# Retention by token tile: decay in the rotary tables, the state summed in PSUM, first network weights loaded during it

## The chip, the core and the metric

The program runs on one core of one Trainium2 chip. The core has five engines that run their own instruction queues and meet only at semaphores: TensorE (PE in the profile; PEld is its loading of stationary operands), VectorE (DVE), ScalarE (ACT), GpSimd (POOL) and SyncE (SP), which here only issues transfers (DMAs). The metric is the device time of one execution in microseconds (us).

## What is computed

`x` is 4 x 512 x 128 float32 (4 batches, 512 tokens, 128 columns). Three parts follow one another: a retention layer with four heads, a local-attention network of six layers, and a second layer (attention and a mixture of experts). The first part is what is rewritten:

```python
xn = layernorm(x)
s, g = retention(xn), silu(network(xn))                 # then x + s * g goes into the second layer
# retention(x), for x = xn:
normed = (x - mu) * rsqrt(var + EPS) * ln_w + ln_b
q, k, v, g = normed @ Wq, normed @ Wk, normed @ Wv, normed @ Wg
q, k = rope(q) * dk ** -0.5, rope(k)                    # dk = 32
def step(S, inp):                                       # per head, over chunks of tokens
    attn = (q @ k.T) * Dmask                            # Dmask = gamma ** (i - j), 0 for j > i
    o = attn @ v + (q * cross) @ S                      # cross = gamma ** (i + 1)
    S = S * gC + (k * kdec).T @ v                       # gC, kdec: powers of gamma
o = o * rsqrt(mean(o ** 2) + EPS) * g_norm_w * silu(g)  # per head
out = x + o @ Wo
```

So there are two norms in a row. The once normed x, transposed, is `state` in the kernel: the retention's product is added to it, and the network starts from it.

## The kernel before, in words

The program is three blocks, one after the other, and every engine meets the others at a barrier between them: `build_retention` (lines 802 to 1206), `build_network` (from 51) and `build_second_layer`.

In the retention, tokens lie 128 to a tile: four tiles (t) of 128 tokens, each for all four batches at once. First come the two norms over all 16 token tiles in two halves (lines 1131 to 1145 on VectorE, 1056 to 1064 on ScalarE), with TensorE transposing x, the once normed x and the twice normed x (954). Then a hardware loop runs over the four tiles; the first three turns are the loop, the last stands behind it. In one turn `project` (982) makes q and k, the gate and v; `rotate` (1163 to 1169) turns q and k and multiplies q by the decay; GpSimd multiplies k by its decay (940) and the gate by the norm weights (944); TensorE transposes q, k and decayed q (990 to 998), makes scores (1012), the state's increment (1003), the product with the state (1021) and the product with v (1027). VectorE applies the decayed mask (1175), blocks out the state's increment (1181) and adds it to the decayed state (1188). ScalarE squares the output (1093), VectorE sums (1185), ScalarE makes the inverse root by Ln and Exp (1095, 1097), VectorE multiplies twice (1190, 1194), TensorE transposes (1036) and multiplies by Wo (1040), VectorE adds `state` (1200). The eight banks of PSUM are four fixed pairs (pa to pd), each reused several times in a turn, so that a step waits until the pair is read out.

In the network's block, SyncE issues the tables and the first layer's weights as its first instructions (220 to 232), GpSimd makes the scaled rotary tables from them (287), VectorE sets constants (666 to 676), and TensorE waits for those constants and for the weights before its first product (384). VectorE's first rotation (716) waits for GpSimd's tables. Each engine's order is written out by hand, stage by stage.

Of the kernel before, what the change touches and what calls it, by code (L numbers as in the profile page):

```python
# [59 lines left out]
def build_network(nc, w_qkv, w_o, w_1, w_2, cols, qk_scale, rotary, win_mask, state):  # L60
# [3 lines left out]
    with ctx:  # L64
# [13 lines left out]
        mask_f = sb("mask_f", [P, 2, 2 * WIN])  # L78
        rot_base = sb("rot_base", [P, 4, TILES, DH])
        rot = sb("rot", [P, 2, 4, TILES, DH])  # L80
        qks = sb("qks", [P, DEPTH * 4, DH])
        wqkv = sb("wqkv", [P, 3 * INNER])
        wo = sb("wo", [P, PAIRS, P])
        w1 = sb("w1", [P, 2 * FF])
        w2 = sb("w2", [P, 3, P])
        col = sb("col", [P, 9])
# [35 lines left out]
        s_const = sig("s_const")  # L122
        s_wq, s_wk, s_wv = sig("s_wq"), sig("s_wk"), sig("s_wv")
        s_qks, s_wo, s_wffn = sig("s_qks"), sig("s_wo"), sig("s_wffn")
        v_moved = [sig(f"v_moved{t}") for t in range(TILES)]
        moves_of = [16 * (16 - 2 * (t == TILES - 1)) for t in range(TILES)]
        c_ident, c_dve, rot_ready = sig("c_ident"), sig("c_dve"), sig("rot_ready")
# [88 lines left out]
        with nc.Block() as block:  # L216

            @block.sync
            def _(sp):
                sp.dma_start(mask_f[:, :, :], win_mask).then_inc(s_const, 16)  # L220
                sp.dma_start(rot_base[:, :, :, :], rotary).then_inc(s_const, 16)

                def load_qkv(l, k, signal):
                    sp.dma_start(half(wqkv, k), w_qkv[l, :, INNER * k:INNER * (k + 1)]).then_inc(signal, 16)

                def load_out(l):
                    sp.dma_start(wo[:, :, :], w_o[l, :, :].rearrange("p (c n) -> p c n", n=P)).then_inc(s_wo, 16)

                def load_ffn(l):
                    sp.dma_start(w1[:, :], w_1[l, :, :]).then_inc(s_wffn, 16)  # L230
                    sp.dma_start(w2[:, :, :], w_2[l, :, :].rearrange("p (c n) -> p c n", n=P)).then_inc(s_wffn, 16)
                    sp.dma_start(col[:, :], cols[l, :, :]).then_inc(s_wffn, 16)

                load_qkv(0, 0, s_wq)
                load_qkv(0, 1, s_wk)
                load_qkv(0, 2, s_wv)
                sp.dma_start(qks[:, :, :].rearrange("p k d -> p (k d)"), qk_scale.to_broadcast([P, DEPTH * 4 * DH])).then_inc(s_qks, 16)
                load_out(0)
                load_ffn(0)

                for g in range(TILE_COUNT):
# [3 lines left out]
                    if last_of_layer:  # L245

                        sp.wait_ge(k_full, 2 * (g + 1))
                        load_qkv(l + 1, 1, s_wk)
                        sp.wait_ge(q_full, 2 * (g + 1))
                        load_qkv(l + 1, 0, s_wq)  # L250
                        sp.wait_ge(v_full, 2 * (g + 1))
                        load_qkv(l + 1, 2, s_wv)
# [13 lines left out]
                    if l > 0 and b == 0 and t == TILES - 1:  # L266

                        sp.wait_ge(wo_full, 2 * r)
                        load_out(l)
                    if l > 0 and b == 1 and t == 2:  # L270

                        sp.wait_ge(x_ffn, 2 * (r - 1))
                        load_ffn(l)

            @block.gpsimd
            def _(pool):
# [4 lines left out]
                pool.wait_ge(s_const, 32)  # L281
                pool.wait_ge(s_qks, 16)

                def tables(l):

                    for k in range(4):
                        ins = nc.gpsimd.tensor_tensor(rot[:, l % 2, k, :, :], rot_base[:, k, :, :],  # L287
                                                      qks[:, 4 * l + k:4 * l + k + 1, :].to_broadcast([P, TILES, DH]), ALU.mult)
                    ins.then_inc(rot_ready, 1)

# [37 lines left out]
                tables(0)  # L328
                for g in range(TILE_COUNT + 2):
# [14 lines left out]
                    if g % (B * TILES) == 2 and l + 1 < DEPTH:  # L344

                        tables(l + 1)
# [455 lines left out]
def build_retention(nc, state, x0T, sT, x, w_ret, w_ro, ret_cols, g_norm, ret_rot, ret_decay, ret_diag, ret_block):  # L802

# [3 lines left out]
    with ctx:  # L807
# [3 lines left out]
        def sig(name, per=1, start=0):  # L811
            return Signal(ctx, nc, name, per, start)


        pa = ctx.enter_context(nc.psum_tensor("pa", [P, 2, 512], F32))
        pb = ctx.enter_context(nc.psum_tensor("pb", [P, 2, 512], F32))
        pc = ctx.enter_context(nc.psum_tensor("pc", [P, 2, 512], F32))
        pd = ctx.enter_context(nc.psum_tensor("pd", [P, 2, 512], F32))

        ident = sb("r_ident", [P, P])  # L820
        eps_col = sb("r_eps_col", [P, 1])
        primer = sb("r_primer", [P, 2])
# [3 lines left out]
        gnw = sb("gnw", [P, 2 * P])  # L826
        rrot = sb("rrot", [P, 2, TILES, RK])
        rdec = sb("rdec", [P, 2, P])
        rdiag = sb("rdiag", [P, RH, P])
        rblock = sb("rblock", [P, 2 * P])  # L830

        xtok = sb("r_xtok", [P, BT, P])
        xc = sb("r_xc", [P, BT, P])
        sqs = sb("r_sqs", [P, BT, P])
        xn = sb("r_xn", [P, BT, P])
        nr = sb("r_nr", [P, BT, P])
        msum = sb("r_msum", [P, BT])
        mean = sb("r_mean", [P, BT])
        vsum = sb("r_vsum", [P, BT])
        var = sb("r_var", [P, BT])  # L840
        lnv = sb("r_lnv", [P, BT])
        rstd = sb("r_rstd", [P, BT])
        nrT = sb("nrT", [P, B, T])

        nrc = sb("nrc", [P, B, P])
        rt1 = sb("rt1", [P, B, 2 * P])
        rt2 = sb("rt2", [P, B, 2 * P])
        rqk = sb("rqk", [P, B, 2 * P])
        qcr = sb("qcr", [P, B, P])
        kst = sb("kst", [P, B, P])  # L850
        vsb = sb("vsb", [P, B, 2 * P])
        sg = sb("sg", [P, B, 2 * P])
        sgn = sb("sgn", [P, B, 2 * P])
        rT = sb("rT", [P, 3, B, P])
        at = sb("at", [P, RH, B, P])
        st = sb("st", [P, B, 2 * P])
        stn = sb("stn", [P, B, 2 * P])
        osq = sb("osq", [P, B, 2 * P])
        oss = sb("oss", [P, B * RH])
        oln = sb("oln", [P, B * RH])  # L860
        orst = sb("orst", [P, B * RH])
        o1 = sb("o1", [P, B, 2 * P])
        o2 = sb("o2", [P, B, 2 * P])
        orT = sb("orT", [P, 2, B, P])

        loads = [(wr[:, :], w_ret), (wro[:, :, :], w_ro), (rcol[:, :], ret_cols), (rrot[:, :, :, :], ret_rot),
                 (rdec[:, :, :], ret_decay), (rdiag[:, :, :], ret_diag), (rblock[:, :], ret_block)]
        all_loads = 16 * (len(loads) + 1)
        c_loads = sig("r_loads")
        r_ident = sig("r_identity")  # L870
        c_set = sig("r_set")
        x_in = [sig("r_x_in_0"), sig("r_x_in_1")]

        steps = sig("r_steps")
        centred = sig("r_centred", 2)
        squared = sig("r_squared", 2)
        stats = sig("r_stats", 2)
        ln_there = sig("r_ln_there", 2)
        rstd_there = sig("r_rstd_there", 2)
# [38 lines left out]
        with nc.Block() as block:  # L918
# [32 lines left out]
            def _(pe):  # L951
# [33 lines left out]
                def retain(t, more):  # L985
# [45 lines left out]
                    if more:  # L1031
                        project(t + 1)
# [1061 lines left out]
```

## Time and profile before

| | us |
|---|---|
| median of 3 runs (1910.48 to 1913.82) | 1913.39 |
| the profiled execution | 1910.66 |
| its span, first to last instruction | 1908.8 |
| PE busy / DVE / ACT / POOL | 1773.3 / 1479.6 / 1179.6 / 1199.0 |

The span is what the trace covers; 1.86 us of the profiled execution's time lie outside it. Busy shares are means over three stages of unlike kind: the retention ends at 133.94 us, the network's steady run lasts until about 1700 us, and the second layer fills the rest. In rows of the timeline, the two first numbers are the start and the duration in us, `xN` counts records, and the bracket gives the idle time before and what ended it. One matrix product in float32 leaves two records in the trace.

### The profile page before, as it was taken

What the parts mean: (1) busy time and instruction counts of PE and PEld (TensorE: products, weight loads), DVE (VectorE), ACT (ScalarE), POOL (GpSimd) and SP (SyncE); (2) the same over time, 40 slices, a digit from 0 to 9 for tenths busy, and PEclk for the clock granted to TensorE, in tenths of its full rate; (3) what the DMA queues carried; (4) which work ended last, traced back from release to release, by engine and by line L of the source; (5) the groups of instructions that cost most, each with busy time, mean ns of one, the idle gap of its engine ahead of it and who ended that gap; (6) DMA issues with size and microseconds to landing.
All of it is one profiled execution on the core that took longest, in us unless ns stands there. A gap on an engine that the chain in (4) does not pass through costs nothing. (4 is left out here: it accounts for less than half of the span.)

```text
span 1908.8 us, 70807 instructions
## 1 busy us (share of the span) xinstructions
PE 1773.3 (93%) x30380; PEld 1139.9 (60%) x30380; DVE 1479.6 (78%) x1676; ACT 1179.6 (62%) x2045; POOL 1199.0 (63%) x1291
## 2 busy tenths in 40 slices
PE   5867899999999999999999999999999999998689
PEld 4743566656665665665566566666656656665356
DVE  6547787887888878788887888888788887876276
ACT  4324666676667657667665766766676666665374
POOL 0108867777776777677677767777776776773000
PEclk9979999999999999999999999999999999999799
DMA  1013322332322322222323223223223222221022
GB/s 50 0 61 91 74 58 66 75 89 67 79 68 58 98 69 73 65 69 66 93 70 77 67 56 103 67 71 78 69 56 91 68 73 72 69 65 27 30 46 67
DMA packets 87379, 128.45 MB, mean 67 GB/s; under 512 B 26616, under 2 KB 32640, under 8 KB 87072
## 3 DMA queue, kind: packets, MB, share of 16 engines
q1 hardware_dynamic: 87072, 123.97, 25.8%
q8 instruction: 240, 3.93, 0.9%
q14 instruction: 67, 0.55, 0.1%
HBM read 25.24 MB, written 1.11 MB: 14 GB/s over the span
## 5 line engine op out<-in xcount | busy, mean ns | idle before, releaser
L317 POOL TENSOR_TENSOR qkn<-t 128x1024 f32<-128x1024 f32 x192 | 453.8, 2364 | 313.1 <-DVE t L720 312.5
L308 POOL TENSOR_TENSOR qkn<-qkn,rn 128x512 f32<-128x512 f32 x384 | 398.2, 1068 | 14.7 <-POOL rn L302 1.3
L444 PEld LDWEIGHTS sc_ps<-prT,v_win 64*64 64x64 f32 x12288 | 198.2, 135 | 147.8 <-issue 146.9
L584 ACT ACTIVATE sq<-qk_ps 128x1024 f32<-128x1024 f32 x192 | 196.0, 1021 | 100.4 <-PE qk_ps L384 98.6
L399 PE MATMUL ring<-ident,qkn 128*128 128x128 f32 x1536 | 242.2, 280 | 10.9 <-POOL qkn L308 10.0
L399 PEld LDWEIGHTS ring<-ident,qkn 128*128 128x128 f32 x1536 | 176.7, 141 | 124.2 <-issue 76.0
L325 POOL TENSOR_TENSOR pn<-pexp,rden 128x512 f32<-128x512 f32 x192 | 196.5, 1045 | 74.2 <-DVE rden L704 74.2
L716 DVE TENSOR_TENSOR t<-qk_ps,rot 128x1024 f32<-128x1024 f32 x192 | 229.4, 1195 | 16.9 <-POOL rot L287 8.6
L577 ACT COPY prT<-ring 128x512 f32<-128x512 f32 x192 | 111.2, 579 | 200.4 <-PE ring L428 199.9
L720 DVE TENSOR_TENSOR t<-qk_ps,rot 128x1024 f32<-128x1024 f32 x192 | 232.9, 1213 | 0.0
L730 DVE TENSOR_REDUCE sums<-sq 128x16 f32<-128x1024 f32 x192 | 232.2, 1209 | 0.0
L444 PE MATMUL sc_ps<-prT,v_win 64*64 64x32 f32 x12288 | 219.2, 221 | 4.1 <-DVE pr L692 3.4
L414 PEld LDWEIGHTS sc_ps<-kT,qT 64*32 64x32 f32 x12288 | 138.1, 105 | 107.5 <-issue 73.6
L374 PE MATMUL qk_ps<-wqkv,state 128*128 128x512 f32 x384 | 197.2, 596 | 0.0
L391 PE MATMUL ring<-wqkv,state 128*128 128x512 f32 x384 | 196.3, 593 | 0.0
L414 PE MATMUL sc_ps<-kT,qT 64*32 64x64 f32 x12288 | 170.3, 224 | 23.7 <-ACT oT L549 12.8
L384 PE MATMUL qk_ps<-wqkv,state 128*128 128x512 f32 x384 | 182.6, 598 | 10.3 <-DMA wqkv<-in_w_qkv 8.5
L683 DVE TENSOR_TENSOR sc_ps<-sc_ps,mask_f 128x1024 f32<-128x1024 f32 x96 | 118.3, 1233 | 86.2 <-PE sc_ps L414 85.4
L459 PE MATMUL ring<-oT,wo 128*128 128x256 f32 x768 | 174.7, 381 | 0.0
L549 ACT COPY oT<-sc_ps 128x512 f32<-128x512 f32 x192 | 112.9, 589 | 70.9 <-PE sc_ps L444 70.9
L459 PEld LDWEIGHTS ring<-oT,wo 128*128 128x128 f32 x768 | 143.0, 191 | 17.7
L738 DVE TENSOR_TENSOR xa<-ring,state 64x256 f32<-64x256 f32 x96 | 40.6, 423 | 136.3 <-PE ring L459 134.9
(223 smaller groups left out, 2808.8 us busy)
## 6 DMA issues: line engine op xcount, KB each, us to landing
v_win<-v_tok SPq DMA_DIRECT2D x1488, 64.0 KB
wqkv<-in_w_qkv SPq DMA_DIRECT2D x18, 512.0 KB, 3.6
spread<-gate_rows SPq DMA_DIRECT2D x32, 128.0 KB, 3.8
wo<-in_w_o SPq DMA_DIRECT2D x6, 512.0 KB, 3.8
w<-in_w SPq DMA_DIRECT2D x6, 341.0 KB, 3.3
w<-in_w SPq DMA_DIRECT2D x6, 192.0 KB, 2.9
r_xtok<-in_x SPq DMA_DIRECT2D x4, 256.0 KB, 3.7
out_x<-xo SPq DMA_DIRECT2D x4, 256.0 KB, 2.2
```

What stands on the lines that cost most here:

```text
L308: nc.gpsimd.tensor_tensor(by_head(quarter(qkn, f)), by_head(quarter(qkn, f)), rn[:, 8 * f:8 * (f + 1)].unsqueeze(2).to_broadcast([P, 8, DH ...
L317: nc.gpsimd.tensor_tensor(half(qkn, k), half(t1, k), half(t2, k), ALU.add).then_inc((q_added, k_added)[k], 1)
L325: nc.gpsimd.tensor_tensor(by_head(quarter(pn, f)), by_head(quarter(pe_, f)), rden[:, 8 * f:8 * (f + 1)].unsqueeze(2).to_broadcast([P, 8, D ...
L374: nc.tensor.matmul(qk_ps[:, f, :], tile_of(g), quarter(wqkv, f), start=True, stop=True).then_inc(q_full, 1)
L391: nc.tensor.matmul(ring_bank("v", g, f), tile_of(g), quarter(wqkv, 4 + f), start=True, stop=True).then_inc(v_full, 1)
L399: ins = nc.tensor.transpose(to[:, n * P:(n + 1) * P], qkn[:, c * P:(c + 1) * P], ident[:, :])
L414: ins = nc.tensor.matmul(sc_ps[WIN * q:WIN * (q + 1), par, 64 * pair:64 * (pair + 1)], qT[64 * par:64 * (par + 1), pair, WIN * q:WIN * (q ...
L444: ins = nc.tensor.matmul(sc_ps[64 * par:64 * (par + 1), part, P * pair + WIN * q:P * pair + WIN * (q + 1)], v_win[64 * part:64 * (part + 1 ...
L459: ins = nc.tensor.matmul(to[:, 0:2 * P], wo[:, c, :], oT[:, c, 2 * P * f:2 * P * (f + 1)], start=(c == 0), stop=(c == PAIRS - 1))
L716: nc.vector.tensor_tensor(by_head(half(t1, k)), by_head(of), rot[:, l % 2, 2 * k, s:s + 1, :].to_broadcast([P, HEADS, DH]), ALU.mult).then ...
L720: nc.vector.tensor_tensor(half(t2, k).rearrange("p (h s d) -> p h s d", s=2, d=DH // 2), swapped, rot[:, l % 2, 2 * k + 1, s:s + 1, :].to_ ...
L730: nc.vector.tensor_reduce(sums[:, HEADS * k:HEADS * (k + 1)], by_head(half(sq, k)), AX.X, ALU.add).then_inc(sums_ready, 1)
```

## The change

The diff changes the first block and moves the first loads of the second. In words:

- The decay powers go into the rotary tables: q's table holds `gamma ** (n - 255.5) * dk ** -0.5`, k's holds the inverse power, for n over all 512 tokens. A plain causal mask replaces the decayed one, and the state needs no decay: its increments are summed in two PSUM banks (`held`) over the tiles, and VectorE only blocks them out into SBUF before each product.
- The norms are made per tile, and the second norm's variance is worked out from the first (`second_variance`). The weights `g_norm_w` are multiplied into Wo once (`scale_weights`). The decay of q and k and the gate's weighting on GpSimd are gone. The sum of the two rotated terms is on VectorE, as before.
- The loop is gone: 36 uses of two pairs of PSUM banks are listed in one order (`fills`), and each engine's queue is written out over all four tiles.
- ScalarE sets the table for Ln and Exp once, at the start; the loads behind it are put in by the build. Line 1091, which set it again in every tile, is gone.
- SyncE issues the network's tables and first weights in the retention's block, and GpSimd makes the first rotary tables there.
- In the second layer two waits (`gated`, `a_max`) become the helper `then`, which waits in the same place on another semaphore.

```diff
+class NetworkWeights:
+    def load_tables(self, sp):
+        sp.dma_start(self.mask_f[:, :, :], self.win_mask).then_inc(self.s_const, 16)
+        sp.dma_start(self.rot_base[:, :, :, :], self.rotary).then_inc(self.s_const, 16)
+        sp.dma_start(self.qks[:, :, :].rearrange("p k d -> p (k d)"), self.qk_scale.to_broadcast([P, DEPTH * 4 * DH])).then_inc(self.s_qks, 16)
...
 def build_retention
+                load_x(0)
+                load_x(1)
+                for to, of in first_loads:
+                    sp.dma_start(to, of).then_inc(c_first.sem, 16)
+                load_x(2)
+                load_x(3)
+                for to, of in later_loads:
+                    sp.dma_start(to, of).then_inc(c_later.sem, 16)
+                weights.load_tables(sp)
+                for k in range(3):
+                    weights.load_qkv(sp, 0, k)
+                weights.load_out(sp, 0)
+                weights.load_ffn(sp, 0)
...
+                def update(t):
...
+                    for b in range(B):
+                        ins = nc.tensor.matmul(held[:, b // 2, 256 * (b % 2):256 * (b % 2 + 1)], rqk[:, t % 2, b, P:2 * P], vsb[:, t % 2, b, :],
+                                               start=(t == 0 and b % 2 == 0), stop=(b % 2 == 1), skip_group_check=True)
...
+                def second_deviation(t):
+                    act.wait_ge(v2_there.sem, t + 1)
+                    nc.scalar.activation(ln2[:, t, :], v2[:, t, :], ACT.Ln, bias=rcol[:, 2:3]).then_inc(logs.sem, 1)
+                    log_taken()
+                    nc.scalar.activation(rstd2[:, t, :], ln2[:, t, :], ACT.Exp, scale=-0.5).then_inc(rstd2_there.sem, 1)
...
+                def inverse_norms(t):
+                    act.wait_ge(r_ms.sem, t + 1)
+                    nc.scalar.activation(oln[:, t % 2, :], oss[:, t % 2, :], ACT.Ln, bias=rcol[:, 2:3], scale=1.0 / RV).then_inc(logs.sem, 1)
+                    log_taken()
+                    if t >= 2:
+                        act.wait_ge(r_o.sem, t - 1)
+                    nc.scalar.activation(orst[:, t % 2, :], oln[:, t % 2, :], ACT.Exp, scale=-0.5).then_inc(r_orst.sem, 1)
...
+                def rotate(t, k):
...
+                    if k == 0:
...
+                        nc.vector.tensor_tensor(rt1[:, :, :], of, table, ALU.mult)
+                    else:
+                        for s in range(2):
+                            ins = nc.vector.tensor_tensor(heads(rt2[:, :, :])[:, :, :, s, :], heads(of)[:, :, :, 1 - s, :], heads(table)[:, :, :, s, :], ALU.mult)
+                        ins.then_inc(r_terms.sem, 1)
+                def add_terms(t):
...
+                    nc.vector.tensor_tensor(rqk[:, t % 2, :, :], rt1[:, :, :], rt2[:, :, :], ALU.add).then_inc(r_rot.sem, 1)
+                def masked(t, k):
...
+                                            rmask[:, :].unsqueeze(1).to_broadcast([P, 2 * B, P]), ALU.mult).then_inc(r_at.sem, 1)
...
 def build_network
-                load_qkv(0, 0, s_wq)
-                load_qkv(0, 1, s_wk)
-                load_qkv(0, 2, s_wv)
-                load_out(0)
-                load_ffn(0)
...
-                tables(0)
```

Three places in the engines' queues show what moves. The first is TensorE's queue in the retention. Before, this is one turn of the loop from the scores on (`at` is the masked scores, `st` the state, `nrc` the normed input, `o` the gated output):

```order
L1012 MATMUL pa<-rT 128x128 x8
L1012 MATMUL pc<-rT 128x128 x8
L1016 REGISTER_ALU
L1003 MATMUL pb<-vsb,kst 128x256 x2
L1021 MATMUL pd<-st,rT 128x256 x4
L1027 MATMUL pd<-vsb,at 128x64 x8
L982 MATMUL pa<-wr,nrc 128x256 x4
L982 MATMUL pc<-wr,nrc 128x256 x4
L982 MATMUL pb<-wr,nrc 128x256 x4
L1036 MATMUL pd<-r_ident,o 128x128 x8
L1040 MATMUL pd<-orT,wro 128x512 x2
```

Now, in the middle of the same engine's queue (`rqk` is rotated q and k, `r_held` the summed state, `nr` and `xn` the twice and once normed x):

```order
L1036 MATMUL r_out_ps<-vsb,at 128x64 x16
L989 MATMUL r_ring<-r_ident,rqk 128x128 x8
L966 MATMUL r_ring<-r_ident,r_nr 128x128 x4
L972 MATMUL r_ring<-r_ident,r_xn 128x128 x4
L1013 MATMUL r_held<-vsb,rqk 128x256 x4
L981 MATMUL r_ring<-wr,nrc 128x256 x12
L1024 MATMUL r_out_ps<-st,rT 128x256 x4
L966 MATMUL r_ring<-r_ident,r_nr 128x128 x4
L981 MATMUL r_ring<-wr,nrc 128x256 x4
```

Before, only the next tile's projection stands between a tile's output and its transposes; now work of three tiles stands there, and a tile's last steps come a tile or more later.

The second is ScalarE's queue at the retention's end. Before, from the last tile's transposed scores' operands to the barrier:

```order
L1090 COPY rT<-pd 128x512 x2
L1090 COPY rT<-pb 128x512
L1091 ACT_TABLE_LOAD
L1093 ACTIVATE osq<-pd 128x1024
L1095 ACTIVATE oln<-oss,r_eps_col 128x16
L1097 ACTIVATE orst<-oln 128x16
L1102 COPY orT<-pd 128x512 x2
L918 UNCONDITIONAL_BRANCH
```

Now, the same stretch (`oln` is the logarithm of the summed squares `oss`, `orst` the inverse root):

```order
L1188 ACT_TABLE_LOAD
L1188 ACTIVATE oln<-oss,rcol 128x16
L1192 ACT_TABLE_LOAD
L1192 ACTIVATE orst<-oln 128x16
L1184 ACTIVATE osq<-r_out_ps 128x1024
L1198 COPY orT<-r_ring 128x1024
L1188 ACT_TABLE_LOAD
L1188 ACTIVATE oln<-oss,rcol 128x16
L1192 ACT_TABLE_LOAD
L1192 ACTIVATE orst<-oln 128x16
L1198 COPY orT<-r_ring 128x1024 x2
L900 UNCONDITIONAL_BRANCH
```

Where one load stood ahead of both functions, one now stands ahead of each; over the retention ScalarE has eleven loads and had nine.

The third is SyncE's queue around the barrier (the branches) between retention and network. Before:

```order
L925 DMA rblock<-in_ret_block 128x256
L926 DMA gnw<-in_g_norm 128x256
L918 UNCONDITIONAL_BRANCH
L218 UNCONDITIONAL_BRANCH
L220 DMA mask_f<-in_win_mask 128x128
L221 DMA rot_base<-in_rotary 128x1024
L224 DMA wqkv<-in_w_qkv 128x1024 x3
L237 DMA qks<-in_qk_scale 128x1536
L227 DMA wo<-in_w_o 128x1024
```

Now:

```order
L914 DMA wro<-in_w_ro 128x256
L914 DMA gnw<-in_g_norm 128x2
L86 DMA mask_f<-in_win_mask 128x128
L87 DMA rot_base<-in_rotary 128x1024
L88 DMA qks<-in_qk_scale 128x1536
L91 DMA wqkv<-in_w_qkv 128x1024 x3
L94 DMA wo<-in_w_o 128x1024
L900 UNCONDITIONAL_BRANCH
L258 UNCONDITIONAL_BRANCH
L281 DMA v_win<-v_tok 32x512
```

All of the network's first loads now stand ahead of the barrier, behind the retention's own loads.

## Rows read from the trace of the kernel before

**Rows 1.** The page: the span, first to last instruction.

```profile
span 1908.8 us, 70807 instructions
```

**Rows 2.** Stretches A:B: length, busy us (records) per engine, PEclk, DMA share, GB/s.

```profile
51.00:74.00 23.00, 19.79 (x131) 16.46 (x130) 14.19 (x14) 8.79 (x12) 4.09 (x2) 1.00 0.00 0
...
120.20:134.00 13.80, 5.75 (x12) 2.73 (x12) 6.15 (x6) 2.68 (x5) 0.00 (x0) 0.62 0.00 0
134.00:147.20 13.20, 6.17 (x11) 2.83 (x12) 1.23 (x8) 2.88 (x4) 3.27 (x6) 0.62 0.81 305
147.20:1700.00 1552.80, 1500.72 (x28084) 947.48 (x28083) 1276.65 (x1359) 1016.13 (x1776) 1145.91 (x1235) 1.00 0.29 72
```

**Rows 3.** Timeline of one tile, 51 to 74 us: start, duration, engine, line, operation.

```profile
51.18 1.02 ACT L1093 ACTIVATE osq<-pd 128x1024 f32<-128x1024 f32 x1 [7.99 <-PE pd L1027]
52.24 1.22 DVE L1185 TENSOR_REDUCE oss<-osq 128x16 f32<-128x1024 f32 x1 [4.53 <-ACT osq L1093]
53.49 0.31 ACT L1095 ACTIVATE oln<-oss,r_eps_col 128x16 f32<-128x16 f32 x1 [1.29 <-DVE oss L1185]
54.06 1.28 ACT L1083 ACT_TABLE_LOAD   x1
55.36 1.02 ACT L1083 ACTIVATE sg<-pc 128x1024 f32<-128x1024 f32 x1
...
57.10 0.86 PEld L1036 LDWEIGHTS pd<-r_ident,o 128*128 128x128 f32 x8 [1.12 <-DVE o L1194]
...
58.92 1.98 PE L1040 MATMUL pd<-orT,wro 128*128 128x512 f32 x4 [0.73 <-ACT orT L1102]
...
61.21 1.40 DVE L1200 TENSOR_TENSOR sT<-pd,state 64x512 f32 x2
...
64.99 1.37 PE L1012 MATMUL pa<-rT 32*128 32x128 f32 x13
...
67.74 1.13 PE L1003 MATMUL pb<-vsb,kst 128*128 128x256 f32 x4
...
68.71 1.89 PE L1021 MATMUL pd<-st,rT 128*128 128x256 f32 x8
...
70.43 3.68 PE L1027 MATMUL pd<-vsb,at 128*128 128x64 f32 x32
73.95 1.95 PE L982 MATMUL pa<-wr,nrc 128*128 128x256 f32 x8
```

**Rows 4.** Timeline of the start, 0 to 36 us.

```profile
4.51 1.22 DVE L1136 TENSOR_REDUCE r_msum<-r_xtok 128x8 f32<-128x1024 f32 x1 [2.36 <-DMA r_xtok<-in_x]
...
12.40 0.17 DVE L1142 TENSOR_SCALAR r_var<-r_vsum 128x8 f32<-128x8 f32 x1
...
16.84 1.92 PE L954 MATMUL pd<-r_ident,r_xn 128*128 128x128 f32 x8
...
24.40 2.35 ACT L1072 COPY state<-pc 64x512 f32<-64x512 f32 x4
...
32.05 3.35 PE L982 MATMUL pa<-wr,nrc 128*128 128x256 f32 x8 [3.53 <-DVE nrc L1152]
```

**Rows 5.** Transfers of the first 12 us: count, KB each, median us from issue to landing.

```profile
wr<-in_w_ret SPq DMA_DIRECT2D x1, 384.0 KB, 4.9
```

**Rows 6.** Timeline of the retention's end and the network's start, 132 to 148 us.

```profile
132.53 1.41 DVE L1200 TENSOR_TENSOR sT<-pd,state 64x512 f32<-64x512 f32 x2 [6.51 <-PE pd L1040]
...
138.34 0.23 DVE L676 TENSOR_SCALAR centre_w<-ident 128x128 f32<-128x128 f32 x1 [2.77 <-DMA rot_base<-in_rotary]
...
141.03 3.47 PE L384 MATMUL qk_ps<-wqkv,state 128*128 128x512 f32 x4 [8.53 <-DMA wqkv<-in_w_qkv]
...
144.34 2.77 POOL L287 TENSOR_TENSOR rot<-rot_base,qks 128x256 f32<-128x256 f32 x4 [9.46 <-DMA qks<-in_qk_scale]
...
147.21 1.22 DVE L716 TENSOR_TENSOR t<-qk_ps,rot 128x1024 f32<-128x1024 f32 x1 [8.64 <-POOL rot L287]
```

**Rows 7.** A stretch at the retention's end, columns as in rows 2.

```profile
123.60:134.00 10.40, 5.75 (x12) 2.73 (x12) 3.76 (x5) 1.17 (x2) 0.00 (x0) 0.50 0.00 0
```

More of the change, by code:

```diff
@@ L63, in build_network @@
+def build_network(nc, weights, state):
     ctx = ExitStack()
@@ L344, in _ @@
                     if g % (B * TILES) == 2 and l + 1 < DEPTH:
-                        tables(l + 1)
+                        weights.scale_rotary(nc, l + 1)
             @block.tensor
@@ L851, in build_retention @@
[L851 to L863, printed above, removed]
@@ new lines, in turn_qk, with scores @@
+                def turn_qk(t):
+                    pe.wait_ge(r_rot.sem, t + 1)
+                    free("turn", t)
+                    for k in range(2):
+                        for b in range(B):
+                            ins = nc.tensor.transpose(banks_of("turn", t)[:, k, P * b:P * (b + 1)], rqk[:, t % 2, b, P * k:P * (k + 1)], ident[:, :])
+                    ins.then_inc(r_turned.sem, 1)
+                def scores(t, k):
+                    if k == 0:
+                        pe.wait_ge(r_T.sem, t + 1)
+                    what = ("low", "high")[k]
+                    free(what, t)
+                    for h in (2 * k, 2 * k + 1):
@@ L1065, in _ @@
-                for n, banks in ((1, (pc, pd)), (2, (pa, pb))):
-                    for half in range(2):
-                        act.wait_ge(turned.sem, turned.at(n, half + 1))
-                        for b in range(2 * half, 2 * half + 2):
-                            if n == 1:
-                                for late, rows in enumerate(HALVES):
-                                    first = b * SHIFTED + late
-                                    ins = nc.scalar.copy(state[rows, first:first + T], banks[half][rows, b % 2, :])
-                            else:
-                                ins = nc.scalar.copy(nrT[:, b, :], banks[half][:, b % 2, :])
-                        ins.then_inc(copied.sem, 1)
@@ new lines, in copy_state @@
+                def copy_state(t):
+                    act.wait_ge(s_turned.sem, t + 1)
+                    if t == 0:
+                        act.wait_ge(c_set.sem, B)
+                    for late, rows in enumerate(HALVES):
+                        ins = nc.scalar.copy(state[rows, :].rearrange("p (b n) -> p b n", b=B)[:, :, P * t + late:P * (t + 1) + late],
+                                             banks_of("ln", t)[rows, 1, :].rearrange("p (b n) -> p b n", b=B))
+                    ins.then_inc(s_copied.sem, 1)
```

812 lines of the change are left out of this document (487 added, 325 removed).

## The prediction

> **What bounds the kernel now.** I read the page first [rows 1], then the busy time by stage, since shares over the whole span mix three stages. In the network's steady stretch TensorE is busy 1500.72 of 1552.80 us [rows 2]: nothing there is touched, and a network that starts earlier ends earlier by the same time. The retention is another case. It ends at 132.53 + 1.41 = 133.94 us [rows 6], and one of its tiles takes 23.00 us, of which TensorE is busy 19.79, VectorE 14.19 and ScalarE 8.79 [rows 2]. The timeline of that tile shows why TensorE isn't full: squares (51.18), sum (52.24), Ln (53.49), two products on VectorE, transposes (57.10), Wo (58.92), the sum with `state` (61.21) run one behind the other on four engines, each engine waiting for the last [rows 3]. Behind the last tile stand 13.80 us with TensorE busy for 5.75 [rows 2]. Ahead of the first tile stand 32.05 us of norms. Then the network waits for its own loads: its first product is at 141.03, behind 8.53 us of idleness that ended with the transfer of `wqkv`, its first rotation at 147.21, behind GpSimd's tables, which waited for `qks` [rows 6].
>
> **The change part by part: the retention.** Every tile's work now lies beside that of two others, so I take the durations of the old rows and lay them out in the new queues, each instruction behind its engine's last one and behind what it waits for, with 0.05 us for a signal between engines. TensorE's prices at the pace of the tile in rows 3, from start to start: a group of four 128x256 products (a projection, the state's increment, the product with the state) 70.43 - 68.71 = 1.72; the 16 score products 67.74 - 64.99 = 2.75; the 16 products with v 73.95 - 70.43 = 3.52; eight transposes 0.86; the two products with Wo 1.72 (four records at 0.43, the 1.98 less the tail of the last). VectorE: 1.22 per 1024 columns, 0.70 per 512 (two in 1.40), 0.17 for a small one [rows 3, 4]. ScalarE: 1.02 per 1024, 0.59 per 512 (four in 2.35), a table load 1.28, Ln 0.31 [rows 3, 4].
>
> First, up to the first dense stretch of TensorE. Tile 0 of x is there at about 4.4 (4.51 before, for two transfers [rows 4]). Mean, centring and square to 7.0; VectorE centres tile 1 meanwhile, then variance, root, second variance and second root to 10.1; VectorE is then busy with tile 2, and the twice normed tile stands at 11.9. Transposes and copy to 13.9, and q and k by 17.9, at the low pace (below). Rotation with its sum, and tile 1's norm among it, to 22.4; transposes of q and k wait for a copy of `state` on ScalarE until 25.1, and tile 0's v starts at 26.5, when tile 1's q and k are read out of the bank that it wants. Tables and weights of the retention do not hold this up: the last that tile 0 needs is issued as the sixth transfer, at about 3.3, and with the 4.9 us of `wr` [rows 5] lands by about 8.2, near the first Ln.
>
> Second, the dense stretch, from tile 0's v to tile 3's product with v. The queue holds ten projections (17.2), eight half-tiles of scores (11.0), four products with v (14.1), three increments and three products with the state (10.3), three transposes of q and k (2.6), tiles 2 and 3 normed (1.7), one transposed output (0.9) and one Wo (1.7): 59.5. Waits that the other engines cause in it: 0.3 + 0.4 + 0.2 + 0.5 + 0.2, together 1.5. VectorE has about 16 us of work per tile and ScalarE 13 with its loads, where TensorE has 18.7, so neither is late for long. End: 26.5 + 59.5 + 1.5 = 87.5.
>
> Third, the tail. ScalarE squares the last tile to 89.2, copies tile 1's output to 90.2, loads a table to 91.5, Ln, loads another, Exp to 93.3, copies tile 2's output to 94.4. Wo of tile 2 and transposes of tile 3 to 97.2, copy to 98.3, Wo to 100.3, two sums to 101.8. The tail, 14.3 us, is as long as before: the two loads that stand in it take what the overlap gives. So the retention ends at 101.8 instead of 133.94: 32.1 us off.
>
> **Clock.** At the start, eight transposes took 1.92 at 16.84 and a projection 3.35 at 32.05 [rows 4], against 0.86 and 1.72 in the tile [rows 3]: that is 1.2 GHz against 2.4. Behind the last tile, after TensorE had waited since 120.2, the granted clock was 0.50, the lower level [rows 7]. I take the low level for all of TensorE's work until 17 us, when the first projection is through. If the low pace lasted until 30 us, the same layout ends at 107.0; with the high one from the start, at 99.2. The Trainium skill, page "TensorE: Matmul & The Clock Gate", Part 4 "PE-mode transpose", says that transposes don't count as busy time for that clock. The trace agrees as far as it goes: transposes that followed others without a gap still ran at the low pace [rows 4]. By that rule the many transposes in the new start would keep the low pace longer, which is the 107.0; it is rival B.
>
> **ScalarE's loads.** The change has two more loads, but what counts is where they stand: one between Ln and Exp, in the chain. The load took 1.28 and the next operation began 0.02 behind its end [rows 3]. With no cost for loads the layout ends at 99.5, with twice the row, as if the engine had to empty first, at 110.6. The page "ScalarE: Activation LUTs" of the Trainium skill, section "What ACT_TABLE_LOAD costs", gives a load of about 1.28 us and as much again for draining, about 2.66 together. I go by the row; the page's price is rival C.
>
> **The network's start.** What remains ahead of the first product is VectorE's constants. They were done at 138.34 - 2.77 = 135.57 (the idle time before `centre_w` [rows 6]), 1.63 behind the retention's end; with `centre_w` (0.23) and a signal TensorE starts 1.91 behind it instead of 7.09. Four records at the low pace take 3.47 as before [rows 6], and the squares 1.02, so the first rotation comes 6.5 behind the end instead of 147.21 - 133.94 = 13.3: 6.8 off. At the high pace it would be 8.5. I take the low pace, since TensorE has waited 3 us by then, in a thin tail. GpSimd's 2.77 us of tables lie in the retention, where GpSimd has only four other operations. Transfers: 3.9 MB queue behind the retention's own and stand in nobody's way, since the retention's own are issued first; its last table tile is wanted at 24 us. Bounds: 0 (they land too late) to 8.5.
>
> **Second layer.** The two waits keep their places and what they wait for: 0. Beside the network nothing else changes: its queues are those of before, with other line numbers.
>
> **Sum.** 32.1 + 6.8 = 38.9 off. Against the profiled execution's own time (the span of 1908.8 [rows 1] and 1.86 outside it, 1910.66) that is 1871.8; that execution lies 2.7 below the median of the runs, from which the sum gives 1874.5. I say 1873.
>
> **Rivals.**
> A, the layout holds, with a microsecond or three more or less in the waits between engines: 1870 to 1877. Chance 0.70.
> B, TensorE stays at the low level until the dense stretch at 30 us: 5.2 later, 1878. For it: its work comes in short pieces in the first 25 us, much of it transposes. Against: a projection of 3.4 us and transposes stand together at 12 to 17 us. 0.10.
> C, each table load costs twice its row: 8.8 later, 1882. Against it stands the row. 0.04.
> D, the change doesn't do what it says at the barrier: the network's first rotation still comes 13 us behind the retention, because something else than loads is late there. 6.8 later, 1880. For it: two waits, TensorE's for `wqkv` and GpSimd's for `qks`, ended at different times, so a third may lie under them. Against: constants are all that is left in the queues. 0.06.
> E, the high level from the start and at the network's start: 2.6 and 1.7 earlier, 1869. 0.06.
> F, slower than before: TensorE holds the low level through the retention, as its work now waits in small pieces on other engines. Then TensorE's queue alone sets the time and the retention ends at 168.3, 66.5 later: 1939. It decides once the low pace lasts until about 100 us, where the layout ends at 140.4, the 133.94 plus what the network's start gives back. Against it: the old tile, with TensorE busy for 19.79 of 23.00, kept a granted clock of 1.00 [rows 2], and the new stretch is denser. 0.04.
>
> **How the numbers follow.** 1873 is A's. The range 1863 to 1888 takes in B to E, and room for signals that cost 0.1 us rather than 0.05 (2 us later) or waits with several signals. A difference under 0.2% (3.8 us) can't be told from none here. All but F are far below 1909.6: faster 0.95, no change 0.01, slower 0.04.
>
> **What would show it.** Right: the last sum into `sT` ends at 100 to 104 us; from 26 to 87 TensorE has no gap over 1 us; the four tiles' products with v end near 35, 59, 70 and 88 us; Ln and Exp of a tile with 1.28 between them; the first rotation 6 to 7 us behind the retention's end with no wait on a transfer. Wrong: granted clock at 0.50 past 30 us, gaps over 1 us in the dense stretch that end with VectorE or ScalarE, or a network whose steady stretch is not 1553 us long.

## The result, and the profile after

The changed kernel takes 1883.59 us (median of four runs, 1881.55 to 1887.45) against 1912.72 of the kernel before (four runs): ratio 0.9852, 95% interval 0.9837 to 0.9867. That is 29.1 us off, where the forecast had 38.9 by its sum and 1873 as its number. The profiled run is the longest of the four, 1887.45.

The page of the changed kernel, the row that answers to [rows 1]:

```profile
span 1885.3 us, 70702 instructions
```

The end of the retention and the network's start, changed kernel (start us, us, engine, line, operation), answering to [rows 6]:

```profile
102.52 1.28 ACT L1188 ACT_TABLE_LOAD   x1
103.81 0.31 ACT L1188 ACTIVATE oln<-oss,rcol 128x16 f32<-128x16 f32 x1
104.14 1.28 ACT L1192 ACT_TABLE_LOAD   x1
...
112.65 1.41 DVE L1355 TENSOR_TENSOR sT<-r_ring,state 64x512 f32<-64x512 f32 x2 [2.55 <-PE r_ring L1054]
...
116.07 3.14 PE L392 MATMUL qk_ps<-wqkv,state 128*128 128x512 f32 x4 [3.46 <-DVE centre_w L684]
...
120.47 1.23 DVE L724 TENSOR_TENSOR t<-qk_ps,rot 128x1024 f32<-128x1024 f32 x1 [4.49 <-ACT sq L592]
```

The last sum into `sT` ends at 112.65 + 1.41 = 114.06, against 133.94 before and 101.8 forecast. The network's first product now waits for VectorE's `centre_w` and for no transfer, and its first rotation comes 120.47 - 114.06 = 6.41 behind the retention's end, where it was 13.27. So the network starts its rotations 147.21 - 120.47 = 26.7 us earlier. From there to the last masked score of the network (1726.92 here, 1750.73 before) the two profiles need 1606.45 and 1603.52, and from that score to the end of the span 158.4 and 158.1: the second layer neither gained nor lost. This also accounts for the span: 26.74 - 2.93 - 0.31 = 23.50, and 1908.8 - 1885.3 is the same. The 2.93 is not put down to the change: the network's queues are the same, and this stretch took 1596.34 to 1602.67 in the seven profiles of the experiments. So it differs by up to 10 us from profile to profile, which is as large as most differences between the experiments' times; these are therefore read by where the retention ends. The two profiled executions lie 23.2 apart and the medians 29.1; no run shows where the rest lies.

The retention, then, kept 12.3 us of what the forecast took off. TensorE's stretches by granted clock (columns as in [rows 2]; a stretch with a mean between 0.5 and 1 is in part at each level), changed kernel:

```profile
20.40:24.40 4.00, 3.22 (x8) 2.59 (x9) 3.14 (x6) 1.23 (x3) 0.83 (x1) 0.59 0.20 64
34.60:41.50 6.90, 6.90 (x34) 6.81 (x34) 0.88 (x3) 2.51 (x3) 0.00 (x0) 0.51 0.00 0
58.70:72.00 13.30, 13.30 (x57) 12.36 (x57) 4.53 (x4) 2.00 (x3) 0.00 (x0) 0.50 0.00 0
```

TensorE's queue through the dense stretch, changed kernel. The lines are: L981 a projection, L1001 the score products, L1036 the products of masked scores with v, L1045 transposes of the output:

```profile
27.51 1.89 PE L981 MATMUL r_ring<-wr,nrc 128*128 128x256 f32 x8
29.33 2.88 PE L1001 MATMUL r_ring<-rT 32*128 32x128 f32 x32
32.55 5.03 PE L1036 MATMUL r_out_ps<-vsb,at 128*128 128x64 f32 x32 [0.33 <-DVE at L1318]
...
55.41 2.88 PE L1001 MATMUL r_ring<-rT 32*128 32x128 f32 x32
58.53 2.94 PE L1001 MATMUL r_ring<-rT 32*128 32x128 f32 x16 [0.24 <-DVE at L1318]
61.40 7.09 PE L1036 MATMUL r_out_ps<-vsb,at 128*128 128x64 f32 x32
...
79.08 3.68 PE L1036 MATMUL r_out_ps<-vsb,at 128*128 128x64 f32 x32
...
84.83 2.79 PE L1001 MATMUL r_ring<-rT 32*128 32x128 f32 x32 [0.32 <-ACT rT L1178]
87.92 1.96 PE L981 MATMUL r_ring<-wr,nrc 128*128 128x256 f32 x8 [0.30 <-DVE at L1318]
...
96.62 3.68 PE L1036 MATMUL r_out_ps<-vsb,at 128*128 128x64 f32 x32
100.14 1.04 PE L1045 MATMUL r_ring<-r_ident,og 128*128 128x128 f32 x8
```

Two things are to be seen. TensorE has no gap over 0.33 us from 27.51 to 100.14, as forecast. And in two stretches, 34.6 to 41.5 and 58.7 to 72.0, it worked at the lower of its two levels (granted clock 0.51 and 0.50, 1.2 GHz) although it was busy for 6.90 of 6.90 and 13.30 of 13.30 us. The products with v show it best: 7.09 us at 61.40, 3.68 at 79.08 and 96.62, for the same 16 products (32 records). Before each fall stood score products (32 rows of 128) and a wait of 0.33 or 0.24 us for VectorE's mask. The first fall began two microseconds into the products with v, the second already at the start of the scores at 58.53, ahead of its products with v. The run of scores at 84.83 has a projection behind it, and no fall.

### The profile page after: what moved, and what is told of

It reads as the page before. It is cut to its first block and busy times, and to the rows that moved or that the text cites. A ratio compares the mean times of both kernels' runs of the same rounds, so it can differ in the third digit from the quotient of the medians.

```text
span 1885.3 us, 70702 instructions
## 1 busy us (share of the span) xinstructions
PE 1779.3 (94%) x30348; PEld 1144.3 (61%) x30348; DVE 1460.8 (77%) x1677; ACT 1179.7 (63%) x2045; POOL 1185.2 (63%) x1287
## 5 line engine op out<-in xcount | busy, mean ns | idle before, releaser
L317 POOL TENSOR_TENSOR qkn<-qkn,rn 128x512 f32<-128x512 f32 x384 | 396.9, 1064 | 14.3 <-POOL rn L311 0.9
L407 PE MATMUL ring<-ident,qkn 128*128 128x128 f32 x1536 | 243.2, 281 | 10.7 <-POOL qkn L317 10.1
L422 PE MATMUL sc_ps<-kT,qT 64*32 64x64 f32 x12288 | 171.0, 224 | 28.1 <-issue 13.9
```

What stands on the lines that cost most here:

```text
L317: nc.gpsimd.tensor_tensor(by_head(quarter(qkn, f)), by_head(quarter(qkn, f)), rn[:, 8 * f:8 * (f + 1)].unsqueeze(2).to_broadcast([P, 8, DH ...
L407: ins = nc.tensor.transpose(to[:, n * P:(n + 1) * P], qkn[:, c * P:(c + 1) * P], ident[:, :])
L422: ins = nc.tensor.matmul(sc_ps[WIN * q:WIN * (q + 1), par, 64 * pair:64 * (pair + 1)], qT[64 * par:64 * (par + 1), pair, WIN * q:WIN * (q ...
```

## The experiments

Theory 1: the clock falls in these stretches because of the kind and order of TensorE's work, the score products above all. Theory 2: it falls because of the short waits there. In the code, `scores(t, k)` are a half-tile of scores, `update(t)` the state's increment and `attend(t)` the products with v, with tiles counted from 0: `attend(1)` is the second tile's. Times are compared by their ratio to the kernel before, run on the same chip: 1911.4 us beside four of the kernels, 1913.94 beside the three called filled, first half and all together. The changed kernel's ratio is the 0.9852 (0.9837 to 0.9867) of the section before.

**Scores over all rows.**

```
- matmul(... rT[rows, t % 2, 1, b, :], rT[rows, t % 2, 0, b, :], ...)
+ matmul(... rT[:, t % 2, 1, b, :], rT[:, t % 2, 0, b, :], ...)
```

> Changed against the kernel after: each of the 16 score products of the retention reads all 128 rows of the turned q and k instead of the 32 rows of its head, so the scores are sums over four heads. Everything else stands. Theory 1 (the granted clock falls at 34 to 42 and 58 to 72 us because of the kind of work there, the score products of 32 rows with what surrounds them, although TensorE is busy): the clock stays at 1.00 through both stretches, attend(1) takes 3.7 us instead of 7.1, and the retention ends 8 to 11 us earlier than the 114.1 us of the kernel after, at 103 to 106. Theory 2 (it falls because of the waits of 0.3 to 0.4 us on other engines that lie in those stretches): the waits remain, the clock falls as before, and the end stays at 113 to 117.

Measured: 1873.96 us, ratio 0.9809 (0.9794 to 0.9824). The kernel leaves out the split of the scores by head, so its output is another. Two stretches of this kernel, and TensorE's scores of the first tile and products with v of the second:

```profile
34.00:42.00 8.00, 8.00 (x57) 7.56 (x57) 3.04 (x6) 5.25 (x7) 0.00 (x0) 1.00 0.00 1
58.00:66.00 8.00, 8.00 (x53) 7.43 (x53) 5.07 (x6) 2.15 (x3) 0.00 (x0) 1.00 0.00 0
```

```profile
29.30 3.73 PE L1001 MATMUL r_ring<-rT 128*128 128x128 f32 x32
...
57.63 3.68 PE L1036 MATMUL r_out_ps<-vsb,at 128*128 128x64 f32 x32
```

The clock stays at 1.00 in both, the products take 3.68, and the last sum ends at 103.95 + 1.41 = 105.36, 8.7 us earlier, although the scores themselves are dearer (3.73 us for a tile's 32 records instead of 2.88). The waits are gone too, since the longer scores cover them, so this run speaks for theory 1 without yet excluding theory 2.

**The same work in another order.**

```
  scores(0, 1)
+ update(0)
  attend(0)
  ...
- update(0)
  ...
- update(1)
  turn_qk(2)
  scores(1, 0)
  scores(1, 1)
+ update(1)
  scores(2, 0)
```

(VectorE's `state_rows(2)` moves behind `masked(1, 1)` with it.)

> Same work as the kernel after in another order: the state update of the first tile stands between its scores and its products with the masked scores, and the second tile's update stands between its second scores and the third tile's first scores, with VectorE's state rows for the third tile behind the second tile's masks. Theory 1 (the clock falls where products of few rows or columns and transposes follow each other in one long run): 128-row products of the update break the run, the clock stays up longer, and the retention ends 4 to 10 us earlier than 114.1. Theory 2 (waits): the waits of TensorE hardly change, and the end stays within 2 us of 114.1.

Measured: 1873.43 us (five runs, 1873.05 to 1875.15), ratio 0.9803 (0.9790 to 0.9816), 9 to 10 us under the changed kernel with the same operations. TensorE's queue and two stretches of this kernel:

```profile
31.79 1.99 PE L1013 MATMUL r_held<-vsb,rqk 128*128 128x256 f32 x8
33.62 3.68 PE L1036 MATMUL r_out_ps<-vsb,at 128*128 128x64 f32 x32
37.14 1.04 PE L989 MATMUL r_ring<-r_ident,rqk 128*128 128x128 f32 x8
...
51.92 1.06 PE L989 MATMUL r_ring<-r_ident,rqk 128*128 128x128 f32 x8 [1.83 <-ACT state L1157]
...
55.73 1.99 PE L1013 MATMUL r_held<-vsb,rqk 128*128 128x256 f32 x8
...
59.29 3.79 PE L1036 MATMUL r_out_ps<-vsb,at 128*128 128x64 f32 x32
```

```profile
34.00:42.00 8.00, 7.64 (x58) 6.97 (x58) 2.17 (x4) 4.60 (x6) 0.00 (x0) 1.00 0.00 0
58.00:73.00 15.00, 15.00 (x109) 13.65 (x107) 9.82 (x10) 4.35 (x4) 0.00 (x0) 1.00 0.01 2
```

The clock is 1.00 in both stretches and the last sum ends at 105.28 + 1.41 = 106.69, 7.4 us earlier. TensorE waits more than in the changed kernel (1.83 us for ScalarE at 51.92, right before the transposes and scores of the second tile), and no fall follows. L1013 is the state's increment, in its new places. So a wait in this stretch does not by itself bring a fall. That says nothing of the low stretch of the start: each of these profiles has one between 18 and 26 us, behind waits of 2.11 and 0.87 us, and what brings it about was not tested.

**The short waits filled.**

```
+ if k == 1 and t < 2:
+     for b in range(B):
+         ins = nc.tensor.matmul(...)   # the last head's four products again
  ins.then_inc(r_sc.sem, 1)
```

> Changed against the kernel after: the last four score products of the first and of the second tile are issued twice (the same values written again, 0.35 us each time), so that the 0.33 us that TensorE waits for VectorE's mask at 32.2 and the 0.24 us at 58.3 are filled with work of the same kind. Theory 1 (kind and order of the work): the clock falls in both stretches as before, within 2 us of the same places, and the whole stays within 3 us of the kernel after. Theory 2 (the short waits): without them the clock holds, attend(1) takes 3.7 us instead of 7.1, and the retention ends 8 to 11 us earlier, near the kernel with the spread order (1873).

Measured: 1880.46 us, ratio 0.9831 (0.9801 to 0.9862), which can't be told from the changed kernel's. TensorE's products with v of the first two tiles, and stretches of this kernel:

```profile
32.92 5.36 PE L1039 MATMUL r_out_ps<-vsb,at 128*128 128x64 f32 x32
...
60.61 5.72 PE L1039 MATMUL r_out_ps<-vsb,at 128*128 128x64 f32 x32
```

```profile
34.00:42.00 8.00, 8.00 (x43) 7.96 (x42) 1.78 (x5) 2.30 (x3) 0.00 (x0) 0.57 0.00 1
58.00:66.00 8.00, 8.00 (x65) 7.88 (x61) 4.27 (x4) 2.03 (x4) 0.00 (x0) 0.76 0.00 0
```

Neither place has a wait any more (TensorE works from 26.49 to the first fall without one), and the clock falls in both stretches all the same: products with v of 5.36 and 5.72 us instead of 3.7. Theory 2 is out as the cause. Theory 1 had the second fall within 2 us of its old place and the whole within 3; the fall began 3.5 us later and was shorter, the whole is 3.1 under, and the last sum ends at 109.91 + 1.41 = 111.32. Whether the wait has a part in how long a fall lasts stays open.

**Only the first half of the new order.**

```
  scores(0, 1)
+ update(0)
  attend(0)
  ...
- update(0)
```

> Of the spread order only its first half: the state update of the first tile stands between its scores and its products with the masked scores. The rest stands as in the kernel after. Theory 1: the clock holds at 34 to 42 us and still falls behind the second and third tile's scores, at about 55 to 70; the retention ends about 3 to 4 us earlier than 114.1 and the whole is 3 to 4 us under the kernel after, at 1879 to 1881. Theory 2 (waits): the 0.24 us behind the second tile's scores remains, so the second fall too, and the first wait is gone: the same. A third theory, that one fall brings on the next: with the first gone the second is gone as well, and the whole comes to 1873 to 1875.

Measured: 1879.21 us, ratio 0.9825 (0.9797 to 0.9852). TensorE's products with v of the first two tiles, the projection behind the fourth tile's scores, and stretches of this kernel:

```profile
33.91 3.68 PE L1036 MATMUL r_out_ps<-vsb,at 128*128 128x64 f32 x32
...
57.93 6.07 PE L1036 MATMUL r_out_ps<-vsb,at 128*128 128x64 f32 x32
...
82.49 3.27 PE L981 MATMUL r_ring<-wr,nrc 128*128 128x256 f32 x8 [0.30 <-DVE at L1318]
```

```profile
34.00:42.00 8.00, 7.64 (x59) 7.03 (x58) 2.46 (x4) 4.31 (x6) 0.00 (x0) 1.00 0.00 0
58.00:66.00 8.00, 8.00 (x39) 7.60 (x39) 2.79 (x3) 1.02 (x1) 0.00 (x0) 0.57 0.00 0
```

The first tile's products with v take 3.68, the second's 6.07: the first fall is gone where the order was changed and the second stands where it was not. The third theory is out: the second fall does not need the first. The last sum ends at 108.90 + 1.41 = 110.31, 3.8 earlier, as expected of theory 1; the interval of the whole time overlaps the changed kernel's. A further, short fall came at 83 to 86 us, 0.5 us into the projection behind the fourth tile's scores (3.27 us instead of 1.96). The changed kernel and five others have the same instructions there and no fall, so full products right behind the scores don't exclude one.

**The network's loads behind the retention again.**

```
@block.sync of the retention:
- weights.load_tables(sp); load_qkv (3); load_out; load_ffn   # to the network's start
@block.gpsimd of the retention:
- weights.scale_rotary(nc, 0)                                 # to the network's start
```

> Undone in the kernel after: the network's first weights, its tables and GpSimd's scaling of the rotary tables stand behind the retention again, as in the kernel before. If the forecast's term holds, TensorE's first rotation on VectorE comes 13.3 us behind the retention's end instead of 6.4, so the whole is 6.9 us longer than the kernel after. A rival: the weight loads and GpSimd's work beside the retention slow it (VectorE's rotation of the first tile 1.98 us instead of 1.22), so that the retention ends 1 to 3 us earlier here and the whole is only 4 to 6 us longer.

Measured: 1888.79 us, ratio 0.9873 (0.9857 to 0.9890). The end of the retention and the network's start, this kernel:

```profile
109.45 1.41 DVE L1355 TENSOR_TENSOR sT<-r_ring,state 64x512 f32<-64x512 f32 x2 [2.55 <-PE r_ring L1054]
...
120.09 3.75 PE L400 MATMUL qk_ps<-wqkv,state 128*128 128x512 f32 x4 [10.68 <-DMA wqkv<-in_w_qkv]
...
125.09 1.22 DVE L732 TENSOR_TENSOR t<-qk_ps,rot 128x1024 f32<-128x1024 f32 x1 [9.39 <-ACT sq L600]
```

The first product waits for `wqkv` again and the first rotation comes 125.09 - 110.86 = 14.23 behind the end (109.45 + 1.41), 7.8 more than in the changed kernel: the term is confirmed, a little larger. The whole is only 5.2 longer (4.0 by the ratios, whose intervals overlap), and in the profile the retention ended 3.2 earlier. That is the size that the rival gave, but not by what it said: VectorE's sum of two rotated terms does take 1.23 us instead of 1.98, but it is the second tile's, and TensorE turns that tile's q and k only at 36.20 here and 37.37 there, without a wait. Tile 0's v starts at 27.67 here and 27.51 there. It is the first fall, which this profile does not have; TensorE's first products with v in it:

```profile
32.61 3.76 PE L1036 MATMUL r_out_ps<-vsb,at 128*128 128x64 f32 x32 [0.24 <-DVE at L1318]
```

The products with v take 3.76 us here and 5.03 in the changed kernel, with the same instructions ahead of them on TensorE and the same kind of wait (0.24 us). So in the first place the clock fell in one profile and held in another, and what decides it no run shows.

**Ln and Exp with one load.**

```
  def inverse_norms(t):
+     if t < 2:
+         nc.scalar.preload_act_table_set(LN_EXP_SET)
```

> Added to the kernel after: before the Ln of the first two tiles' head norms the table that holds both Ln and Exp is asked for by name. In the kernel after, the last tiles' norms load a table before each Ln and each Exp, 1.28 us a load, with the next operation 0.02 us behind it. If those loads in the middle of the retention are hidden behind TensorE and only those of the tail stand on its path: the pair at 56.6 and 58.2 becomes one load and the retention's end moves by 0 to -1.3 us. If the load takes more than its row, the end moves by more than that. If the low stretch at 58.7 us comes from a wait of TensorE behind these loads (theory 2), the clock there holds and the end moves by -5 us or more; by theory 1 the low stretch stays.

Measured: 1880.98 us, ratio 0.9840 (0.9827 to 0.9854), an interval that overlaps the changed kernel's. ScalarE in the tail of this kernel:

```profile
95.83 1.28 ACT L1188 ACT_TABLE_LOAD   x1
97.12 0.31 ACT L1190 ACTIVATE oln<-oss,rcol 128x16 f32<-128x16 f32 x1
...
97.58 0.29 ACT L1190 ACTIVATE oln<-oss,rcol 128x16 f32<-128x16 f32 x1
...
98.04 3.68 PE L1036 MATMUL r_out_ps<-vsb,at 128*128 128x64 f32 x32
...
112.19 1.41 DVE L1357 TENSOR_TENSOR sT<-r_ring,state 64x512 f32<-64x512 f32 x2 [2.89 <-PE r_ring L1054]
```

One load serves two tiles: the second Ln stands 97.58 - 97.12 = 0.46 us behind the first, and no load stands behind it. From the start of the last products with v to the end of the last sum it takes 113.60 - 98.04 = 15.56, against 114.06 - 96.62 = 17.44: 1.9 off. That is more than the 1.3 expected at most, yet not because a load takes more than its row: the expectation counted one load, and four begin in the changed kernel's tail (97.56, 99.18, 102.52, 104.14). The last two, 2.56 by their rows, stand on the last tile's path; here ScalarE waits 0.38 there for VectorE's sum. In this profile the first low stretch was longer (products with v of 6.81 us at 32.36, instead of 5.03) and took 1.4 back (the last products with v start at 98.04 instead of 96.62), so the retention's end moved by only 0.5. The low stretch behind the load at 56.6 stayed, as theory 1 has it.

**All of it together.**

```
  the new order, and the named table, and:
- gate(1)
  copy_state(3)
+ gate(1)
```

> The spread order with the table of Ln and Exp asked for by name at the first two tiles' head norms, and with ScalarE's copy of the fourth tile's state ahead of the second tile's gate (TensorE waits 1.83 us for that copy at 50.1 in the spread order). If both gains add to the spread order's 1873.4: the copy gives 0.5 to 1.0 and the loads left out 0.5 to 2.6, so 1870 to 1872.5; if the loads are hidden in the spread order, only the copy's: 1872.4 to 1873.

Measured: 1874.47 us, ratio 0.9796 (0.9771 to 0.9821): no difference from the new order alone (0.9803) can be told, and it lies in neither of the two ranges expected. A stretch of this kernel, its first increment of the state on TensorE, and the two ends of its tail:

```profile
32.00:36.00 4.00, 4.00 (x14) 3.26 (x14) 3.52 (x9) 0.00 (x0) 0.00 (x0) 0.57 0.03 6
```

```profile
32.03 3.65 PE L1013 MATMUL r_held<-vsb,rqk 128*128 128x256 f32 x8
```

```profile
90.70 3.68 PE L1036 MATMUL r_out_ps<-vsb,at 128*128 128x64 f32 x32
...
104.86 1.41 DVE L1357 TENSOR_TENSOR sT<-r_ring,state 64x512 f32<-64x512 f32 x2 [2.90 <-PE r_ring L1054]
```

The tail is shorter by the same 1.9 (106.27 - 90.70 = 15.57), but the clock fell at 32.2 (0.57 from 32 to 36), 0.2 us into `update(0)`, so that `update(0)` took 3.65 us instead of 1.99, 1.7 lost. TensorE's wait for the fourth tile's state is 1.36 us instead of 1.83. TensorE's instructions up to the fall are those of the new order alone, which had none. The new order makes the falls fewer and shorter; it does not exclude them.

**All profiles together.** Whether the clock fell in the two places in each profile, and the mean granted clock of every run of the kernel, over the whole execution with its other stages:

| kernel | first place | second place | mean clock of its runs |
|---|---|---|---|
| changed kernel | fell | fell | 0.976 to 0.979 |
| named table | fell | fell | 0.977 to 0.980 |
| late loads | held | fell | 0.977 to 0.979 |
| waits filled | fell | fell | 0.979 to 0.982 |
| first half of the new order | held | fell | 0.980 to 0.984 |
| all together | fell, shorter | held | 0.980 to 0.984 |
| new order | held | held | 0.984 to 0.986 |
| scores over all rows | held | held | 0.983 to 0.984 |

In the second place the kind and order of the work decide, as far as eight profiles go: with the scores of two tiles in a row the clock fell in five profiles of five; with the increment between them, or with scores of 128 rows, it held in three of three. In the first place there is only a tendency: it fell in three of four profiles with the products with v right behind the scores, and in one of three with the increment between. The runs without a profile agree, as far as a mean over all stages can tell: each of the nine runs of the last two kernels has a higher mean clock than each of the changed kernel's four. No run changed the 64-column products themselves, so their part in it is not shown.

## Why the prediction came out as it did, point by point

**The step that failed** is the one called "Clock": "I take the low level for all of TensorE's work until 17 us, when the first projection is through." Up to there it held (that projection took 3.78 us at 13.76, the low pace). What failed is that everything behind it was priced at the high level. Behind that stood the reading, in rival F, that the old tile "kept a granted clock of 1.00 [rows 2], and the new stretch is denser". The clock was read as a matter of how full TensorE is. In the changed kernel it fell while TensorE was full, and the prediction's own sign of being wrong, "granted clock at 0.50 past 30 us", came true. In the old tile the scores were followed by the state's increment and the product with the state, 128 rows and 256 columns [rows 3]; the change put the 64-column products right behind the first tile's scores, and in the second place the scores of two tiles in a row. With both increments back between them, or with scores of 128 rows, there was no fall in either stretch, but for the one from 32 to 36 us in the run with all together.

**The size of it.** 6.90 us at 0.51 and 13.30 at 0.50 are 20.2 us of work that takes 10.1 at the high level: 10.1 lost. A third low stretch lies in 20.4 to 24.4 us (0.59): the second tile's projection took 3.64 us at 21.18 instead of about 1.9, its transposes and ScalarE's copy of `state` behind it came late, and tile 0's v started at 27.51 instead of 26.5: 1.0. The dense stretch took 100.14 - 27.51 = 72.6 instead of 61.0, of which 10.1 are the clock's and 1.5 are left; the tail took 13.9 instead of 14.3. The sum is 1.0 + 10.1 + 1.5 - 0.4 = 12.2, and the retention ended 114.06 - 101.8 = 12.3 late.

**What held.** The prices from the old tile: 3.5 us from start to start for the products with v (79.08 to 82.60), 1.7 for a projection. The order of the queue and the waits in it: 0.33, 0.24, 0.32 and 0.30, together 1.2 where the forecast had 1.5. The network's start: 6.4 behind the retention's end (6.5 forecast), TensorE's first product 2.01 behind it (1.91), and 7.8 us dearer when undone (6.8). The second layer: 0.

**What was luck.** The measured 1883.59 lies in the range of 1863 to 1888, but the range was drawn above all for rivals B to E, and none of them came. And that the same operations in the new order came to 1873.43, the number of the forecast, does not confirm the layout. Their retention ends at 106.69, 4.9 later than the 101.8, by the waits for ScalarE among others. Their network's first rotation stands 5.22 behind that, not 6.5, since TensorE's first product there ran at the high pace (1.95 us at 108.70). The network's own stretch was 2.6 shorter than before, within its differences from profile to profile.

**ScalarE's loads.** All eleven took 1.28, and behind the eight ahead of Ln and Exp the next operation began 0.01 to 0.02 behind the load's end. Without the four that begin in the tail, two of them (2.56 by their rows) on the last tile's path, the tail was 1.9 shorter. The Trainium skill, page "ScalarE: Activation LUTs", section "What ACT_TABLE_LOAD costs", counts as much again for draining, about 2.66 together; the trace does not agree, and rival C is out.

**The rivals.** A, the layout, missed by the clock. B had the right resource in the wrong place: it held TensorE low until the dense stretch, and the three low stretches begin at 21, 35 and 59 us, two of them inside it. The rule on transposes that stood behind B (the Trainium skill, "TensorE: Matmul & The Clock Gate", Part 4 "PE-mode transpose") does not single out these places: what stood ahead of the falls were scores and products with v, and in the new order eight transposes at 37.14 followed the products with v at a clock of 1.00. D, E and F did not come: the first rotation moved, the start ran at the low pace, and the falls were over after 7 and 13 us.

## What to carry to other kernels

Before a dense stretch is priced at the high clock, look at what kind of work it strings together, not only at how full the engine is: here score products of 32 rows, in a row with other short ones, ran into falls that cost 10 of the 39 us forecast, with TensorE busy throughout. Two moved lines of TensorE's queue (and one of VectorE's), which put full products between them, took 7.4 us off the retention without taking out any work. And a profile of one execution tells whether the clock fell in it, not whether it will: the same instructions fell in one run and held in another.

## What had not been expected of the hardware

TensorE's clock fell to 0.50 although the engine had had no wait for 8 us (from 26.49, in the run with the waits filled), and with scores of 128 rows in place of 32, or with the state's increment between, it held in the second place. Which property of the chip this is, and why the first place fell in some profiles and not in others with the same instructions ahead of it, stays open.

GpSimd beside VectorE, the changed kernel and then the one with the late loads:

```profile
27.17 1.04 POOL L931 TENSOR_TENSOR r_xn<-r_xc,r_rstd 128x512 f32<-128x512 f32 x1 [2.56 <-ACT r_rstd L1138]
27.31 1.98 DVE L1309 TENSOR_TENSOR rqk<-rt 128x1024 f32<-128x1024 f32 x1
28.17 3.77 POOL L104 TENSOR_TENSOR rot<-rot_base,qks 128x256 f32<-128x256 f32 x4
```

```profile
27.11 1.23 DVE L1309 TENSOR_TENSOR rqk<-rt 128x1024 f32<-128x1024 f32 x1
27.33 1.91 POOL L934 TENSOR_TENSOR r_xn<-r_xc,r_rstd 128x512 f32<-128x512 f32 x1 [2.60 <-ACT r_rstd L1138]
```

In the first, GpSimd's product began 0.14 us ahead of VectorE's sum of two tensors and took 1.04; the sum took 1.98, and GpSimd's tables, which met its rest, 3.77 instead of 2.77 [rows 6]. In the second the sum began first and took 1.23, and the same product 1.91. So the one that came second took longer, by about what was left of the other. The Trainium skill, page "SBUF — State Buffer", section "Who interferes with whom", says so of a VectorE instruction with two inputs in SBUF beside a GpSimd instruction that reads SBUF; the trace agrees, at 0.75, 0.87 and 1.00 us lost. TensorE did not wait for it: it turns that tile's q and k at 37.37, behind other work.
